# An AdaLN block with routed experts: the last four tiles summed on the array, and five down products per tile

## The reference

```python
sa, ca, ga, sb, cb, gb = (silu(c) @ wmod) in six parts, per batch
ga, gb = sign * max(|.|, 0.25)
x = x + ga * attention(layernorm(x) * (1 + ca) + sa)      # 16-wide scale, two softmaxes, one projection
h = layernorm(x) * (1 + cb) + sb
scores = softmax(h @ gate_weight.T)                       # 8 experts in 4 groups, 2 groups kept
topk_w, topk_i = the two best scores in the kept groups
routed = sum over the 2 experts of w * (silu(h @ g_e.T) * (h @ u_e.T)) @ d_e.T     # F = 176 features
shared = (silu(h @ sg.T) * (h @ su.T)) @ sd.T                                      # FS = 352 features
out = x + gb * (routed + shared)
```

## Time and profile before

| | |
|---|---|
| median of 3 runs | 291.94 us (290.74 to 292.01) |
| the profiled execution's own time | 291.79 us |
| its span, first to last instruction | 290.0 us |
| time outside the span | 1.79 us |
| granted TensorE clock, mean of the span | 0.976 |
| busy share PE, PEld, DVE, ACT, POOL | 89%, 82%, 66%, 56%, 44% |

### The profile page before, as it was taken

One profiled execution on the slowest core, in us unless ns is written; L12 is line 12 of the kernel. 1 busy time (PEld: TensorE's weight loads), 2 busy tenths in 40 slices (PEclk: granted clock), 3 DMA queues, 4 the chain that ended last, 5 costly groups with the idle time before them and its releaser, 6 DMA issues.

```text
span 290.0 us, 6198 instructions
## 1 busy us (share of the span) xinstructions
PE 257.4 (89%) x1820; PEld 237.6 (82%) x1820; DVE 190.3 (66%) x579; ACT 161.2 (56%) x429; POOL 128.4 (44%) x146
## 2 busy tenths in 40 slices
PE   0899999898999999999999689999999999999900
PEld 0797688897889989888899579989999999999700
DVE  1675875139988581883697864745555467868893
ACT  2438568878467564747354554446566565656500
POOL 3120404654181078848972855203444454544630
PEclk9999999999999999999999999999999999999955
DMA  7894015341442013142320225344334485584464
GB/s 237 278 347 95 0 32 194 111 122 66 109 112 74 3 57 122 45 126 76 79 108 11 84 92 180 107 125 146 113 129 129 132 254 162 183 251 149 132 189 141
DMA packets 29319, 36.98 MB, mean 128 GB/s; under 512 B 4468, under 2 KB 23903, under 8 KB 29288
## 3 DMA queue, kind: packets, MB, share of 16 engines
q1 hardware_dynamic: 24056, 27.19, 32.3%
q0 software_dynamic: 3408, 8.46, 7.8%
q10 hardware_dynamic: 1824, 0.94, 1.1%
HBM read 24.78 MB, written 12.71 MB: 129 GB/s over the span
## 4 chain that ended last, share of the span: by engine, by line
PE 75%; DVE 7%; issue 5%; ACT 4%; DMA 3%; POOL 3%; ACTq 1%; SPq 0%; DVEq 0%; POOLq 0%
PE bank L343 17%; PE bank L345 17%; PE bank L344 16%; PE bank L1138 4%; PE bank L1353 3%; PE bank L1375 3%; PE bank L1110 3%; PE bank L1130 2%; PE bank L1093 2%; PE bank L1121 2%; PE bank L1102 2%; PE bank L1011 1%; DMA mh<-routed_out 1%; PE bank L540 1%; DMA routed_in<-h2all,slot_u 1%
## 5 line engine op out<-in xcount | busy, mean ns | idle before, releaser
L1441 POOL DMA_INDIRECT routed_out<-yo_all,dest x39 | 40.1, 1028 | 54.8 <-ACT yo_all L1402 35.5
L343 PE MATMUL bank<-experts_w,h2T_lo 128*128 (+1 forms) x156 | 50.6, 325 | 0.1
L345 PE MATMUL bank<-experts_w,h2T_hi 128*128 (+1 forms) x156 | 47.2, 303 | 0.0
L344 PE MATMUL bank<-experts_w,h2T_hi 128*128 (+1 forms) x156 | 47.0, 301 | 0.0
L706 POOL DMA_INDIRECT routed_in<-h2all,slot_u x32 | 31.5, 986 | 23.5 <-DVE slot_u L687 13.3
L1430 DVE SCALAR_TENSOR_TENSOR wstage<-wstage,wt,bank 128x176 f32<-128x176 f32 x39 | 15.5, 397 | 27.9 <-ACT wstage L1392 27.9
L343 PEld LDWEIGHTS bank<-experts_w,h2T_lo 128*128 128x128 f32 (+1 forms) x156 | 29.6, 190 | 0.5 <-issue 0.5
L344 PEld LDWEIGHTS bank<-experts_w,h2T_hi 128*128 128x128 f32 (+1 forms) x156 | 29.7, 190 | 0.0
L345 PEld LDWEIGHTS bank<-experts_w,h2T_hi 128*128 128x128 f32 (+1 forms) x156 | 29.4, 188 | 0.0
L343 PE MATMUL bank<-h2T_hi,wsgu_lo 128*128 128x256 f32 (+1 forms) x96 | 27.9, 290 | 1.5 <-issue 1.5
L345 PE MATMUL bank<-h2T_hi,wsgu_hi 128*128 128x256 f32 (+1 forms) x96 | 27.1, 282 | 1.1 <-issue 1.1
(11 more groups left out here) (248 smaller groups left out, 760.6 us busy)
## 6 DMA issues: line engine op xcount, KB each, us to landing
h2all<-routed_in SPq DMA_DIRECT2D x39, 130.0 KB, 2.2
wstage<-gu_t SPq DMA_DIRECT2D x8, 352.0 KB
res<-x SPq DMA_DIRECT2D x4, 512.0 KB, 9.0
mx<-modrow SPq DMA_DIRECT2D x8, 256.0 KB, 3.7
mh<-modrow SPq DMA_DIRECT2D x8, 256.0 KB
exchange<-routed_out SPq DMA_DIRECT2D x8, 256.0 KB
wmod_s<-w_mod SPq DMA_DIRECT2D x3, 512.0 KB, 9.7
wstage<-down_t SPq DMA_DIRECT2D x8, 176.0 KB
```

Source lines behind the costliest of these rows:

```text
L343: pe.matmul(out_ap, l[1], r[0], start=start, stop=False)
L344: pe.matmul(out_ap, l[0], r[1], start=False, stop=False)
L345: return pe.matmul(out_ap, l[0], r[0], start=False, stop=stop)
L1441: pool.indirect_dma_start(out=routed_out, out_offset=bass.IndirectOffsetOnAxis(dest[:, t % 16:t % 16 + 1], 0), in_=yo[t % 6], in_offset=No ...
```

## The change

Down product. The 176 features are no longer cut 88 + 88 but 128 + 48. The 48 stand at the end of a 64-wide slice (features 112 to 175, the first 16 of the slice, already in the first part, meet weights of zero). The activations of the second part are kept with hi in partitions 0 to 63 and lo in 64 to 127, and the weights of the second part stand twice, in both halves. So hi x hi and lo x hi of the second part are one product over 128 partitions (L1396 of the changed kernel), and hi x lo one over 64 partitions (L1395): five products for six. DVE makes the two lo parts in two operations (L1471, L1472). Each expert's down weights come in by three DMAs for one, and the zero rows are written once by POOL (`pool_stage_rows`).

Last four tiles. Tiles 35 to 38 hold rows of the last batch only. Their results are not scattered: they are split into hi and lo (`yh`, `yl`) and multiplied by one-hot matrices, made by DVE from the token numbers (`dve_row_of`), into one PSUM bank that collects the last batch's 256 x 256 sums (`pe_tile_sum`, four products of 256 columns a tile). SP writes zeros into the last batch's rows of `routed_out` beforehand, and its rows are loaded when 35 tiles are written.

Final steps. For batches 2 to 7 gate x shared and its sum with `res` are done in the loop's steps 3 to 14 (`gated`). The gates of batches 4 to 7 have buffers of their own and are loaded behind tiles 8 to 11. Of the rest (sum, scale, out of each batch) 14 steps stand in the loop at other places, batch 5 is done by POOL, and the last batch is done in halves behind the sum (`final_last`). Some semaphores are shared to make room; with that, two waits are joined: on the router's and the shared expert's weights (`act_later`), and on the last two loads of x (`dve_ln1_stats`).

```diff
-    FH = F // 2
+    HALF = P // 2
+    FB = F - P
+    GAP = HALF - FB
...
                 sp.dma_start(staged("sgu").rearrange("p (k n) -> p k n", k=KD),
-                             sh_gu_t.rearrange("(k p) n -> p k n", p=P)).then_inc(s_wsgu_in, 16)
+                             sh_gu_t.rearrange("(k p) n -> p k n", p=P)).then_inc(s_wrt_in, 16)
...
-                dve.wait_ge((s_x0_in, s_x1p_in, s_x2p_in, s_x3p_in)[p], 16)
+                dve.wait_ge((s_x0_in, s_x1p_in, s_x2p_in, s_x2p_in)[p], 16 if p < 2 else 32)
...
-                sp.dma_start(wstage[r][0:FH, W1:].rearrange("p (j n) -> p j n", j=2),
-                             down_t[ds(e, 1)].rearrange("o (j p) n -> p (o j) n", p=FH)).then_inc((s_est0_in, s_est1_in)[r], 16)
+                if e < 2:
+                    sp.wait_ge(s_const, 18 + e)
+                down = down_t[ds(e, 1)].rearrange("o f n -> f (o n)")
+                for to, of in ((wstage[r][:, W1:W1 + D], down[0:P]), (wstage[r][GAP:HALF, W1 + D:], down[P:F]),
+                               (wstage[r][HALF + GAP:P, W1 + D:], down[P:F])):
+                    sp.dma_start(to, of).then_inc((s_est0_in, s_est1_in)[r], 16)
...
             def pe_tile_act(pe, t, r):
                 pe.wait_ge(s_ea_ready, t + 1)
-                for j in range(2):
-                    last = pe.transpose(ATb[r % 2][0:FH, j * P:(j + 1) * P], av[r % 2][:, j * FH:(j + 1) * FH], ident[:])
+                pe.transpose(ATb[r % 2][:, 0:P], av[r % 2][:, 0:P], ident[:])
+                last = pe.transpose(ATb[r % 2][0:HALF, P:2 * P], av[r % 2][:, F - HALF:F], ident[:])
                 last.then_inc(s_eat_done, 1)
 
             def pe_tile_down(pe, experts, t, r):
                 e = expert_of(pe, experts, r)
                 pe.wait_ge(s_ea_lo, t + 1)
-                for j in range(2):
-                    last = mm3(pe, EDN[r % 2][:, 0:D], parts(avT[r % 2], slice(None), j),
-                               (expert(e, 2, j * D, D), expert(e, 3, j * D, D)), j == 0, j == 1)
-                last.then_inc(s_edn_done, 1)
+                to, (hi, lo) = EDN[r % 2][:, 0:D], avT[r % 2]
+                mm3(pe, to, (hi[:, 0], lo[:, 0]), (expert(e, 2, 0, D), expert(e, 3, 0, D)), True, False)
+                pe.matmul(to, hi[0:HALF, 1], expert(e, 3, D, D, HALF), start=False, stop=False)
+                pe.matmul(to, hi[:, 1], expert(e, 2, D, D), start=False, stop=True).then_inc(s_edn_done, 1)
+
+            SUMMED = 2 * S * (B - 1) // P + NE - 1
...
+            def pe_tile_sum(pe, t):
+                i = t - SUMMED
+                pe.wait_ge(s_ey_lo, i + 1)
+                if i == 0:
+                    pe.wait_ge(s_ex_lo, NT)
+                for n, (j, half) in enumerate(itertools.product(range(TT), (yl, yh))):
+                    last = pe.matmul(Z[:, j * D:(j + 1) * D], row_of[i][:, j * P:(j + 1) * P], half[:, i % 2, :],
+                                     start=(i == 0 and n == 0), stop=(t == NT - 1 and n == 2 * TT - 1), skip_group_check=True)
+                last.then_inc(s_esum_done, 1)
...
-                dve.tensor_tensor(avT[q][1], bank2(ATb[q], P)[0:FH], avT[q][0].bitcast(F32), ALU.subtract).then_inc(s_ea_lo, 1)
+                hi, lo = avT[q]
+                dve.tensor_tensor(lo[:, 0], ATb[q][:, 0:P], hi[:, 0].bitcast(F32), ALU.subtract)
+                dve.tensor_tensor(hi[HALF:P, 1], ATb[q][0:HALF, P:2 * P], hi[0:HALF, 1].bitcast(F32), ALU.subtract).then_inc(s_ea_lo, 1)
+
+            def dve_row_of(dve, t):
+                dve.wait_ge(s_const, 20)
+                tile_landed(dve, t)
+                dve.tensor_scalar(row_of[t - SUMMED], token_ramp, xt_in[t % 8][:, D + 3:D + 4], None, ALU.is_equal)
+
+            def dve_tile_sum(dve, t):
+                i = t - SUMMED
+                dve.wait_ge(s_ey_ready, t + 1)
+                if i >= 2:
+                    dve.wait_ge(s_esum_done, i - 1)
+                dve.tensor_tensor(yl[:, i % 2, :], EDN[t % 2][:, 0:D], yh[:, i % 2, :].bitcast(F32), ALU.subtract).then_inc(s_ey_lo, 1)
...
-            DONE_BY = [15, 15, 23, 23, 31, 31, 35, 39]
+            DONE_BY = [15, 15, 23, 23, 31, 31, SUMMED, SUMMED]
...
+            BY_POOL = (5,)
+            GATED = [(b, step) for b in range(2, B) for step in ("gate", "add")]
+            ROWS = [(b, step) for b in range(B - 1) if b not in BY_POOL for step in ("sum", "scale", "out")]
+            LAST = [(B - 1, step) for step in ("sum", "late0", "late1", "scale0", "scale1", "out0", "out1")]
...
-                    sp_final_gate(sp, 4)
-                    sp_final_gate(sp, 5)
                     store(sp, 0)
                     store(sp, 1)
+                    store(sp, 2)
                     for b in (4, 5):
                         load_rows(sp, b, 0)
                         load_rows(sp, b, 1)
-                    sp_final_gate(sp, 6)
-                    store(sp, 2)
-                    sp_final_gate(sp, 7)
-                    load_rows(sp, 6, 0)
-                    load_rows(sp, 6, 1)
                     store(sp, 3)
-                    load_rows(sp, 7, 0)
+                    for b in (6, 7):
+                        load_rows(sp, b, 0)
+                        load_rows(sp, b, 1)
+                    store(sp, 4)
                     store(sp, 6)
...
-                    FIN_AT = (22, 23, 24, 25, 26, 27, 31, 32, 33, 34, 35, 36, 37, 38)
+                    GATED_AT = tuple(range(3, 3 + len(GATED)))
+                    FIN_AT = (20, 21, 22, 23, 24, 25, 28, 29, 30, 31, 32, 33, 35, 36)
+                    ROW_OF_AT = (33, 34, 35, 36)
```

More of the change, by code:

```diff
@@ L1287, in adaln_block, with expert @@
             pad = exchange[:, 4 * ROW:5 * ROW]
-            def expert(e, part, at, n):
+            def expert(e, part, at, n, rows=P):
                 base = (0, W1, 2 * W1, 2 * W1 + W2)[part]
-                return experts_w[0:(P if part < 2 else FH), ds(e * WE + (base + at), n)]
+                return experts_w[0:rows, ds(e * WE + (base + at), n)]
             def bank2(t, n=256):
@@ L1504, in adaln_block, with gated @@
-            FINALS = [(b, step) for b in range(B) for step in range(fin_all(b))]
+            def gated(dve, b, step):
+                if step == "gate":
+                    gate_landed(dve, b)
+                    dve.wait_ge(s_og_ready, b + 1)
+                    dve.tensor_tensor(og_buffer(b), og_buffer(b), gate_of(b), ALU.mult).then_inc(s_fin, 1)
+                else:
+                    fin_wait(dve, b, "gate")
+                    dve.tensor_tensor(res[:, b], res[:, b], og_buffer(b), ALU.add).then_inc(s_fin, 1)
@@ new lines, in final @@
+            def final(eng, b, step):
+                y0, y1 = y_in[b % 4]
+                done = s_pool_fin if b in BY_POOL else s_fin
+                if step == "sum":
+                    eng.wait_ge(y_sems[b % 4], 32 * (b // 4 + 1))
+                    eng.tensor_tensor(y0[:], y0[:], y1[:], ALU.add).then_inc(done, 1)
+                elif step == "scale":
+                    gate_landed(eng, b)
+                    fin_wait(eng, b, "sum")
+                    eng.tensor_tensor(y0[:], y0[:], gate_of(b), ALU.mult).then_inc(done, 1)
+                else:
+                    if b < 2:
+                        eng.wait_ge(s_res_ready, 2)
+                    else:
+                        fin_wait(eng, b, "add")
+                    fin_wait(eng, b, "scale")
+                    eng.tensor_tensor(res[:, b], res[:, b], y0[:], ALU.add).then_inc(done, 1)
@@ L1650, in _ @@
                     pool_scatter(pool, 3, 7)
-                    for t in range(NT):
+                    pool_token_ramp(pool)
+                    for t in range(SUMMED):
                         pool_tile(pool, t)
+                    for b in BY_POOL:
+                        for step in ("sum", "scale", "out"):
+                            final(pool, b, step)
                 @block.scalar
@@ L2038, in _ @@
                     steps(one)
-                    for b, step in FINALS[len(FIN_AT):]:
+                    dve_tile_sum(dve, NT - 2)
+                    dve_tile_sum(dve, NT - 1)
+                    for b, step in ROWS[len(FIN_AT):]:
                         final(dve, b, step)
+                    final(dve, *LAST[0])
+                    for b, step in LAST[1:]:
+                        final_last(dve, step)
                 @block.tensor
```

143 lines of the change are left out of this document (92 added, 51 removed).

## The result

The changed kernel takes 297.02 us (median of 4 runs, 295.95 to 297.81) against 291.98 us for the kernel before beside it (290.74 to 294.14): ratio 1.0162, 95% interval 1.0091 to 1.0234. Forecast were 282.1 us; rival B gave 296.9. The profiled execution took 297.81 us, its span is 295.9.

The account below looks back on a forecast made before the run. PE's list was taken to bound the loop. 290.0 - 4.6 (down product) + 0.74 (sums) put PE's end at 271.0, DVE's at 278.05, span 280.3; + 1.79 gave 282.1 us, range 279.5 to 297.0.

Parts of the forecast that it names:

- rival B: Down product: the product over 64 partitions (L1395) breaks PE's flow on both sides, price 15.2 us, time 296.9 us; chance 0.23.
- What bounds the kernel: Tile loop: PE's list is the time, 2.11 us a step, 39 steps, with no PE idle.
- I take 0, since of the rows with fp32r none pays: Down product: the new 64-partition fp32r product was taken to cost nothing extra, within bounds of 0 and 15.6 us.
- rows 8 and 9: Profile rows of plain float32 products with 8 columns or 8 rows: entering or leaving costs about 0.2 us each way.
- the late rows: Tail: rows of batches 6 and 7 reach DVE late by 0 to 1.2 us, taken as 0.4.
- The down product's gain: Tile loop: one of six products goes in 39 tiles, 39 x 0.118 = 4.6 us, period 1.99 us.
- DVE's second lo operation: Tile loop: two lo operations of 128 columns for one of 256, 0 to 0.33 us more, taken as 0.07, beside PE.
- The sums and the tail: Last four tiles: sums add 0.74 us, PE's last down product ends at 271.0, DVE at 278.05, span 280.3.
- rival D: Faster by less: DVE late at the end by its lists, or loop gaps behind the second lo operation, 284 to 290.4; chance 0.08.
- the forecast's own range: Whole kernel: 279.5 us to 285.5 us (rows 1.2 late, store slower, one or two late DVE steps in the loop).
- two named terms: Low end of 279.5 us: rows never late (0.4 us taken) and sums hidden (0.74 us taken).
- The early edits at nothing: Zero-row DMAs, extra weight DMAs, joined waits, gated steps and one-hot builds: all taken to cost nothing.

Follow-up runs that it names:

- before_cols64: The kernel before with one of its six down products (hi x lo of the second 88 features) cut to 64 columns: 291.63 us, ratio 1.0012.
- before64: The kernel before with one of its six down products (hi x lo of the second 88 features) cut to 64 partitions: 303.37 us, ratio 1.049.
- two64: The changed kernel with its last down product narrowed to 64 partitions too, beside the other narrow one: 295.83 us, ratio 1.0155.
- before72: The kernel before with one of its six down products (hi x lo of the second 88 features) cut to 72 partitions: 289.09 us, ratio 0.9995.
- full_rows: The changed kernel with the second part's hi x lo product over 128 partitions instead of 64: 281.61 us, ratio 0.9681; measured again, ratio 0.9726.
- five_alone: The kernel before with the five down products alone, hi x lo over 128 partitions, none of the tail's part: 283.95 us, ratio 0.986.
- pool_two: full_rows with batch 6 also given to POOL, its rows loaded behind the last batch's: 283.8 us, ratio 0.984 against the kernel before.

## Why the prediction was wrong, point by point

**What bounds the kernel: right.** PE's list is the loop's time in every variant; the periods of 1.99, 2.11, 2.38 and 2.50 us follow from PE's list alone, even with DVE at 19.2 of 19.9 us.

**The step that failed: "I take 0, since of the rows with fp32r none pays".** The price of the 64-partition product was bounded by 0 and 15.6 us, and I took the lower end. Measured: 0.39 us a tile, 15.2 us in 39, the price that rows 8 and 9 gave (0.2 a change). The working weighed the type over the direction. The earlier trace rows is fp32r but narrow in columns; the earlier trace rows is plain float32 but narrow in partitions, as the new product is. before_cols64 and before64 set these apart in one place of one kernel: 64 columns nothing, 64 partitions 0.39 us. In fp32r narrow columns say nothing about narrow partitions. The rule of the Trainium skill weighed there ("TensorEngine Tiling (Array Packing)", section "Key Properties": a change of tiling mode drains TensorE) fits both, if a product over 64 partitions is a mode of its own: two64 pays once for two narrow products, before72 pays nothing. That a drain is what takes the 0.39 us, no trace here shows. Had I given it the weight of a row, B would have been the forecast.

**Rival B: right in mechanism and place; in size close, in part by luck.** 296.9 forecast, 297.02 measured; the start of L1396 behind L1395 0.31 us (said 0.3), period 2.38 (said 2.4), PE's last down product ending at 286.27 (271.0 + 15.2 = 286.2). I gave it a chance of 0.23. B also let the late rows fall away, and they did not (below): the profiled execution took 297.81, 0.9 above B, and the median hides this.

**The down product's gain: right, 4.6 us.** Period 1.99 in full_rows as forecast; five_alone's ratio gives 4.0 us with an interval that holds it. DVE's second lo operation cost more than I took. In a step of full_rows:

```profile
262.93 0.28 DVE L1471 TENSOR_TENSOR h2T_lo<-bank,h2T_hi 128x128 fp32r<-128x128 f32 x1
263.23 0.28 DVE L1472 TENSOR_TENSOR h2T_hi<-bank,h2T_hi 64x128 fp32r<-64x128 f32 x1
263.54 0.42 DVE L1440 TENSOR_TENSOR h2T_lo<-bank,h2T_hi 128x256 fp32r<-128x256 f32 x1
```

The two advance by 0.61 us (262.93 to 263.54) where one of 256 columns advances by 0.33: 0.28 more, near the bound of 0.33, not the 0.07 that I took from the tail's half steps. It lay beside PE, as said.

**The sums and the tail: right in kind, the exact fit partly luck.** The forecast of 282.1 us is what full_rows gives the first time: 281.61, and 282.7 from the ratio; the second measurement's ratio, 0.9726, makes it 284.0. From the end of PE's last down product to DVE's end it takes 6.5 us in full_rows (270.90 to 277.36), where 7.05 was worked out: the rows of batches 6 and 7 were not late, and the 0.4 us taken for it falls away. In the last steps 1.1 us was lost on PE that the sum did not have: a one-hot build beside POOL's batch 5 took 1.17 us for 0.35, and the sum's copy and lo part stood behind it. That is a piece of rival D, in another place than I looked for it. The last down product ended at 270.90 in spite of it, near the 271.0 of the forecast, since the loop began 1.9 us earlier in that execution than in the one of the kernel before (below), which makes up for it; in the second full_rows it ended at 272.35. The low end of the forecast's own range, 279.5, is 1.5 us below what its two named terms give (282.1 - 0.4 - 0.74 = 281.0).

**In the changed kernel itself** the late rows, which B was to take away, stayed: batch 7's rows came 0.90 us late, since batch 6's load began at 283.49, 4.3 us behind tile 34's scatter (279.22), outside the 2.4 to 3.7 that I had from two rows, and batch 7's only at 284.67.

**The early edits at nothing: not disproved.** The first activation transposes of the loop start at 193.99 in the changed kernel and at 194.14 before; two runs of full_rows have 192.26 and 193.90, so differences below some 2 us there can't be told from the runs' own spread.

## What to carry to other kernels

In a dense list of fp32r products, keep every one over all partitions, or at least (here) 72: pad with zeros, or let the spare partitions carry a harmless term, as lo x lo here. The product over 72 partitions saved nothing, and one over 64 cost 0.39 us for going in and out together; several that must be narrow belong side by side. Before work moves to POOL at a kernel's end, add the 5.6 us of its closing drain to the end of its last operation. When a new form stands in no row, take the price from the row that shares its geometry, and ask of a rule and a row that speak against each other whether they differ in the same direction as the new form does.

## What the runs showed of the hardware

- fp32r products of 256 columns: starts 0.118 us apart over 72, 88 and 128 partitions; with one over 64 among them 0.39 us is lost in the group, and the same 0.39 with two.
- 64 columns of the stationary operand cost nothing, in fp32r (before_cols64) and in a plain float32 transpose (217.01 to 217.12), unlike plain float32 of 8 columns.
- DVE operations on SBUF go from 0.35 to 1.07 and 1.17 us (one-hot build, 128x256) and from 0.38 to about 1.0 (half steps, 128x256) beside a POOL operation of 512 columns; a half step that reads PSUM kept its 0.38. Of two 128x512 steps L1570 that meet, DVE's took 0.68 and POOL's 1.75 for its usual 1.3 in full_rows_b, 0.86 and 1.54 in onehot_early.
- The drain that closes POOL's list ended 5.6 us behind POOL's last 128x512 operation, whether that ended at 270.08 (full_rows) or 274.60 (pool_two); there it set the end of the span.
